# Attention part of a decoder layer: low context parts and the input's addition by accumulating transfers, three context buffers, another order of the norm statistics

## What is computed

```python
x = _layernorm(x + rwkv(x, ...))            # 4 layers with a scan over time
x = _layernorm(x + xattn(x, ctx, ...))      # the part that the change touches
x = _layernorm(x + experts(x, ...))         # 8 experts, gated

def xattn(x, y):                            # 16 heads of 16 channels
    q = softmax(heads(x @ Wq.T + bq))       # over the 16 channels of a head
    k = softmax(heads(y @ Wk.T + bk))
    v = heads(y @ Wv.T + bv)
    D_inv = 1 / sum(q * sum(k over rows))
    out = q + einsum(q, einsum(k, v)) * D_inv
    return out @ Wp.T + bp
```

## The kernel before

| slot n % 4 | DVE between `block_diagonals` and `k_normalise` | DVE behind `low_context` |
|---|---|---|
| 0 | `add_input(n / 4)`: L1164 `x<-x,xin`, then `stats(1, ...)` L1149; in slot 0 the five instructions of `output_bias` ahead of it | `rsqrt(1, ...)` (five instructions, L1155 to L1159), then `denominators` (L1187 `drec`, from slot 4 on) |
| 1 | | `attend`, `q_arguments` |
| 2 | `q_normalise` | in slots 6, 8 and 10 `low_weights` (L1212), in 10 and 14 `low_x2` (L1207) |
| 3 | `add_attention` with its statistics | `rsqrt(2, ...)` |

## Time and profile before

### The profile page before, as it was taken

One profiled execution on the slowest core, in us unless ns is written; L12 is line 12 of the kernel. 1 busy time (PEld: TensorE's weight loads), 2 busy tenths in 40 slices (PEclk: granted clock), 3 DMA queues, 4 the chain that ended last, 5 costly groups with the idle time before them and its releaser, 6 DMA issues.

```text
span 1833.9 us, 27225 instructions
## 1 busy us (share of the span) xinstructions
PE 1733.1 (95%) x10508; PEld 1517.4 (83%) x10508; DVE 1242.6 (68%) x1918; ACT 978.5 (53%) x1505; POOL 3.6 (0%) x26
## 2 busy tenths in 40 slices
PE   3599999999999998998999999999999999999997
PEld 1378888787888788888899889998999989999896
DVE  7999999999999855888544444444454544444446
ACT  4688898898989873444533333233333332333323
POOL 0000000000000000000000000000000000000000
PEclk9799999999999998999999999999999999999999
DMA  4000010001000002111111011110101001020001
GB/s 143 1 24 18 12 47 18 7 7 61 3 12 29 0 29 89 44 55 45 55 35 35 1 35 35 34 34 0 34 34 34 18 16 34 34 74 0 1 1 41
DMA packets 34702, 56.59 MB, mean 31 GB/s; under 512 B 3030, under 2 KB 20412, under 8 KB 33596
## 3 DMA queue, kind: packets, MB, share of 16 engines
q1 hardware_dynamic: 34620, 55.47, 9.3%
HBM read 51.79 MB, written 3.67 MB: 30 GB/s over the span
## 4 chain that ended last, share of the span: by engine, by line
PE 70%; DVE 24%; ACT 3%; issue 2%; DMA 0%; SPq 0%; ACTq 0%; DVEq 0%
PE fbank L1941 33%; PE fbank L1963 17%; PE pair L842 5%; PE pair L802 4%; PE pair L827 3%; DVE kfl L425 2%; PE proj L1435 2%; PE pair L812 2%; DVE st L272 2%; DVE aa L374 1%; DVE bb L370 1%; DVE pp L356 1%; PE pair L792 1%; PE qbanks L1471 1%; DVE x L413 1%
## 5 line engine op out<-in xcount | busy, mean ns | idle before, releaser
L1763 DVE TENSOR_TENSOR hf<-sil,fbank 128x512 f32<-128x512 f32 (+1 forms) x256 | 158.8, 620 | 479.2 <-PE fbank L1941 407.6
L1868 ACT ACTIVATE sil<-fbank 128x512 f32<-128x512 f32 (+1 forms) x256 | 139.2, 544 | 615.1 <-PE fbank L1941 615.1
L1941 PE MATMUL fbank<-xh,wh 128*128 128x512 f32 (+1 forms) x1024 | 289.9, 364 | 1.2 <-ACT sil L1868 1.2
L1941 PE MATMUL fbank<-xl,wh 128*128 128x512 f32 (+1 forms) x1024 | 289.1, 364 | 0.0
L1941 PE MATMUL fbank<-xh,wl 128*128 128x512 f32 (+1 forms) x1024 | 289.0, 363 | 0.0
L1963 PE MATMUL fbank<-wl,hh 128*128 128x256 f32 x896 | 250.4, 279 | 0.0
L1963 PE MATMUL fbank<-wh,hh 128*128 128x256 f32 x896 | 250.3, 279 | 0.0
L1963 PE MATMUL fbank<-wh,hl 128*128 128x256 f32 x896 | 250.2, 279 | 0.0
L1941 PEld LDWEIGHTS fbank<-xl,wh 128*128 128x128 f32 x1024 | 184.6, 189 | 30.8
L1941 PEld LDWEIGHTS fbank<-xh,wl 128*128 128x128 f32 x1024 | 184.5, 189 | 30.4
L1941 PEld LDWEIGHTS fbank<-xh,wh 128*128 128x128 f32 x1024 | 180.5, 189 | 27.8 <-ACT sil L1868 1.6
(11 more groups left out here) (239 smaller groups left out, 3106.0 us busy)
## 6 DMA issues: line engine op xcount, KB each, us to landing
raw<-in_w_gate SPq DMA_DIRECT2D x16, 512.0 KB, 3.9
raw<-in_w_up SPq DMA_DIRECT2D x16, 512.0 KB, 4.8
raw<-in_w_down SPq DMA_DIRECT2D x16, 512.0 KB, 5.7
raw<-in_w_ck SPq DMA_DIRECT2D x4, 1024.0 KB, 4.7
raw<-in_w_cv SPq DMA_DIRECT2D x4, 1024.0 KB, 4.8
raw<-in_ctx_t SPq DMA_DIRECT2D x4, 750.0 KB, 6.3
ct<-in_ctx_t SPq DMA_DIRECT2D x4, 750.0 KB, 4.9
x<-in_x SPq DMA_DIRECT2D x4, 448.0 KB, 6.8
```

The costliest lines, as they stand in the source:

```text
L1763: dve.tensor_tensor(hf[i][:, 0:w], sil[i][:, 0:w], banks(e, t, f)[1][:, 0:w], ALU.mult).then_inc(hf_ready, 1)
L1868: act.activation(sil[f % 2][:, 0:w], banks(e, t, f)[0][:, 0:w], ACT.Silu).then_inc(sil_ready, 1)
L1941: ins = pe.matmul(banks(e, t, f)[k][:, 0:w], m[h][:, o:o + P], a[:, b, columns(c)], start=i == 0, stop=i == 3 * CB - 1)
```

## The change

- The low part of a context is no longer subtracted on DVE. ACT writes the negated high part into `ctl`, and GpSimd issues a transfer that adds the context from HBM onto it (`accum_op=ADD`).
- `cth` and `ctl` have three buffers instead of two. `high_context(n + 3)` stands where `high_context(n + 2)` stood, with `high_context(2)` ahead of it in slot 0.
- `xin` and its loads are gone: GpSimd issues transfers that add the input from HBM onto x in SBUF. DVE's `add_input` becomes `input_stats`, which waits for that transfer and takes the statistics.
- In slots 0, 4, 8 and 12 the statistics stand behind `k_normalise`, and `denominators` stands ahead of `rsqrt(1, ...)`.
- SP waits for `cth_ready` where it waited for `ctl_ready`; `kvbd` takes the place of `xin` in SBUF; the last phase's `eps` waits for `num_done`.

```diff
-        xin = [sb(f"xin{i}", [T, G, C]) for i in range(2)]
+        kvbd = sb("kvbd", [P, 2 * G, CB, P])
...
-        cth, ctl = ([sb(f"{n}{i}", [P, CB, S + 1], F32R) for i in range(2)] for n in ("ach", "acl"))
+        cth, ctl = ([sb(f"{n}{i}", [P, CB, S + 1], F32R) for i in range(3)] for n in ("ach", "acl"))
...
         def gpsimd(pool):
...
+            def add_context(s):
+                pool.wait_ge(minus_ready, s + 1)
+                if s >= 3:
+                    pool.wait_ge(ctl_in[s % 3], 16 * (s // 3))
+                pool.dma_start(ctl[s % 3][:, :, 0:S], io["ctx_t"][:, :, s * S:(s + 1) * S].bitcast(F32R),
+                               accum_op=ALU.add).then_inc(ctl_in[s % 3], 16)
+
+            def add_input(c):
+                if c >= 2:
+                    pool.wait_ge(sum_in[c % 2], 16 * (c // 2))
+                pool.dma_start(x[:, c * G:(c + 1) * G, :], xv[:, c * G:(c + 1) * G, :], accum_op=ALU.add)\
+                    .then_inc(sum_in[c % 2], 16)
+
+            add_context(0)
+            add_context(1)
+            pool.wait_ge(g["x_done"], 2 * STEPS)
+            add_input(0)
+            for s in range(2, B):
+                add_context(s)
+                if s % 2 == 0 and s // 2 < GROUPS:
+                    add_input(s // 2)
...
         def sync(sp):
...
             sp.wait_ge(g["x_done"], 2 * STEPS)
-            load_x(0)
-            load_x(1)
             sp.dma_start(g["wrt"][:], io["wrt"]).then_inc(g["wrt_in"], 16)
...
-                sp.wait_ge(ctl_ready, CG * (j - 1))
+                sp.wait_ge(cth_ready, CG * (j - 1))
                 load_context(sp, io, ct, ct_in, j)
...
         def vector(dve):
...
-            def add_input(c):
-                dve.wait_ge(xin_in[c % 2], 16 * (c // 2 + 1))
-                dve.tensor_tensor(chunk(c), chunk(c), xin[c % 2][:], ALU.add).then_inc(sum_done, 1)
-                dve.wait_ge(sum_done, c + 1)
+            def input_stats(c):
+                dve.wait_ge(sum_in[c % 2], 16 * (c // 2 + 1))
                 stats(1, c)
...
-                    if i == 0 and c1 is not None:
-                        add_input(c1)
                     if i == 2 and c1 is not None:
                         q_normalise(c1)
                     if i == 3 and c2 is not None:
                         add_attention(c2)
                     k_normalise(n)
-                    if n + 2 < B:
-                        low_context(n + 2)
+                    if i == 0 and c1 is not None:
+                        input_stats(c1)
+                    if i == 0 and c2 is not None:
+                        denominators(c2)
                     if i == 0 and c1 is not None:
                         rsqrt(1, c1)
-                    if i == 0 and c2 is not None:
-                        denominators(c2)
...
         def scalar(act):
...
-                if s >= 2:
-
-                    act.wait_ge(proj_done, s - 1)
-                act.activation(cth[s % 2][:, :, 0:S], ct[s // CG % 2][:, :, c0:c0 + S], ACT.Copy).then_inc(cth_ready, 1)
+                if s >= 3:
+
+                    act.wait_ge(proj_done, s - 2)
+                act.activation(cth[s % 3][:, :, 0:S], ct[s // CG % 2][:, :, c0:c0 + S], ACT.Copy).then_inc(cth_ready, 1)
+                act.wait_ge(cth_ready, s + 1)
+                act.activation(ctl[s % 3][:, :, 0:S], cth[s % 3][:, :, 0:S], ACT.Copy, scale=-1.0).then_inc(minus_ready, 1)
...
-                    if n + 2 < B:
-                        high_context(n + 2)
+                    if n == 0:
+                        high_context(2)
+                    if n + 3 < B:
+                        high_context(n + 3)
...
         def tensor(pe):
...
-                pe.wait_ge(ctl_ready, s + 1)
+                pe.wait_ge(ctl_in[s % 3], 16 * (s // 3 + 1))
```

## The result

| | kernel before | changed kernel |
|---|---|---|
| median of 20 runs, us | 1838.33 | 1841.78 |
| lowest, highest | 1835.23, 1839.4 | 1838.97, 1845.22 |
| profiled execution (span) | 1835.63 (1833.9) | 1843.36 (1841.6) |

The ratio is 1.0021 with a 95% interval of 1.0014 to 1.0027: 3.5 us slower, 2.9 us above the predicted 1838.9 and inside the range. 1.0 us of the 7.7 is there before the attention part begins and is no part of the change (0.6 of it by the first instruction on DVE).

What follows compares the result with a forecast made beforehand. PE was taken to bound the kernel, idle about 20 of 190 us. Queues +0.1, input +1.0 and clock 0 gave 1.1 on the profiled 1835.63, 1836.7; 2.2 more to the median made 1838.9 us, range 1832.5 to 1847.

Steps and rivals of the forecast that it cites:

- Slot 0: First attention slot: key quotient starts 2.46 us earlier, PE turns x at 716.5 instead of 717.88; gain 1.4 us.
- Slot 4: denominators ahead of rsqrt makes DVE stand at drec, so PE turns x at 758.45 instead of 756.91; loss 1.54 us.
- Slots 8, 12 and 11: Slots 8 and 12: earlier projection, given back by the order, loss 0.5 us each; slot 11: earlier maximum top, gain 1.0.
- The low parts' transfers: Sixteen accumulating transfers of 375 KB on GpSimd's queue, 8 us each, with enough lead: no cost, bounds 0 to 6.8 us.
- the rival: Slower, by the low parts: 14 us from negation to landing, PE waits before projections of contexts 13 and 5; 1845.7, chance 0.13.
- The input's first part: Slot 0: accumulation issued from 702.59, wanted by DVE at 711.5, taken to land at 712.5; cost 1.0 us.
- The clock: PE's granted clock in slots 0 and 1: gain 2.2 us if no fall, about 2.4 cost if longer; taken as 0.
- The forecast's side: Whole kernel within 0.2% (3.7 us) of the kernel before; chance 0.54.
- The faster one: Freed DVE time reaches PE, moved denominators costs nothing, clock stays up in slot 0: -6.2 us, 1831.6; chance 0.16.
- Input late: Slot 0: the input's first accumulation lands 6 us late, at 717.5, holding DVE at input_stats(0); 1843.9 us, chance 0.17.
- low parts late: Low parts take 14 us instead of 8, so PE waits before projections of contexts 13 and 5; 1845.7 us, chance 0.13.

Runs made afterwards that it cites:

- experiment 8: Experiment 1 with high_context(n + 2) again, so low parts' transfers have a slot less of lead; 1842.67 us beside 1836.63 for the kernel before.
- experiment 1: The changed kernel with denominators put back behind rsqrt(1, ...) in slots 4, 8 and 12; 1833.23 us beside 1837.68 for the kernel before.
- experiment 4: The changed kernel with twelve idle products on PE before its wait for x in slots 4, 8 and 12; 1836.8 us beside 1837.68.
- experiment 5: Experiment 1 with the router's and expert's weights and next context issued only after the input's first part lands; 1832.17 us beside 1836.63.
- experiment 12: The changed kernel again, unedited, on another chip; 1842.82 us beside 1836.85 for the kernel before.
- experiments 9 to 12: Experiment 5 with statistics of groups 1 to 3 earlier (1832.56 us); experiment 1 with input added on DVE (1832.8); the first with slot 0 filled (1828.86); experiment 12 (1842.82).
- experiment 3: The kernel before with denominators ahead of rsqrt and nothing else; 1848.51 us beside 1837.68.
- experiment 2: The kernel before with only the change's order of addition, statistics and denominators, low parts still on DVE; 1848.42 us beside 1837.68.
- experiment 7: Experiment 5 with 24 idle products on PE in slot 0 before the turn of x; 1830.41 us beside 1836.63 for the kernel before.

## Why the prediction came out as it did

**Slot 0** was right to a tenth. With the 1.0 us of start-up taken off, the product starts at 711.6 and the turn at 716.5, as predicted; the fewer idle microseconds before the product came back behind it, 3.28 before the turn.

**Slot 4** was right: turn at 758.40 with the 0.19 by which the product was late taken off, 758.45 predicted. The mechanism is in the rows: DVE stands at `drec` until PE's sums are done, and the five small instructions are queued behind that wait.

**Slots 8, 12 and 11** were right: +0.4 (product of slot 7 to turn of slot 8) and +0.4 instead of +0.5 each, and -1.0. The time that left DVE bought nothing in sum, as said, because each freed piece lies in front of a wait that ends at the same time as before or is given back by the order.

**The low parts' transfers** were right in cost, nothing, and taken too slow: 5.6 us in the median, where 8 was taken and twice the plain load would have been 9 to 15. The issues from 674 to 900 us (KB each, median us from issue to landing), the input's first part by itself, and GpSimd's own time for the first two issues in the part:

```profile
acl<-in_ctx_t POOLq DMA_DIRECT2D x16, 375.0 KB, 5.6
...
x<-in_x POOLq DMA_DIRECT2D x1, 448.0 KB, 6.6
...
703.88 1.24 POOL L1035 DMA_DIRECT2D x<-in_x  x1 [22.64 <-DVE x L463]
...
711.07 1.10 POOL L1028 DMA_DIRECT2D acl<-in_ctx_t  x1 [5.96 <-ACT acl L1335]
```

No projection waited for them. Single ones took longer than the 10 us that the prediction names as a sign of being wrong, 11.1 for a low part and 10.1 for a part of the input, early in the part beside other loads; they had more lead than that. With one slot less of lead the kernel loses 10.5 us (experiment 8), so it is the lead that keeps them free. The Trainium skill's page "SBUF — State Buffer", section "SBUF: two separate sides", on which the rival leaned for a cause, says that GpSimd's descriptor writes stall beside DVE's two-port copies. No run here shows such a stall: sixteen of the twenty issues took 1.05 to 1.24 us. The four others stand right behind another issue and took 1.61 to 1.91, within 0.01 us of that in experiment 1's profile.

**The input's first part** was taken 1.0 us late and in this profile wasn't late at all: 703.88 + 6.6 = 710.5, while DVE came to it at 712.47. In other kernels' profiles it was (9.9 us in experiment 1 with a DVE wait of 1.27, 10.6 in experiment 4); what that costs in the median isn't shown, and experiment 5 puts it near nothing. The pages' estimate, 4.1 us for 448 KB, put together from "DMA: Bandwidth & Descriptors", section "Anatomy of one DMA — SWDGE (gpsimd) path", and "Collectives: The Full Stack", section "The bandwidth ceiling: the fold count and why AG ≠ RS ≠ AR", of the Trainium skill (which gives the halved rate for the reduce-scatter of a ring of cores, not for a transfer like this one), is too short here: 6.0 us even with the other loads held back (experiment 5). The measurement decides.

**The clock is the step that failed.** The prediction took 0 for it, with bounds of -2.2 and +2.4, and looked for it in slots 0 and 1 alone, where the clock was low already. There it moved little (+0.6 up to slot 4). But its own queue model made three new waits of 1.3 us in slots 4, 8 and 12, between two that were there, 0.65 for `drec` and 1.01 for `xt`, and it priced them only as waits. In both profiles of the changed kernel the clock fell behind two of the three: 2.8 us in slots 4 and 5, 1.6 in slots 8 and 9, more than the waits themselves. The rows to size this were in hand: the same turn and projection take 1.76 and 2.05 us at the low level, 0.93 and 1.12 at the high one. Put on slots 4, 8 and 12 that is a bound of 0 to 6.6 us instead of nothing.

The medians fit that. The queues give about 0 (+0.1 predicted, -0.1 read off), and with the waits filled the changed kernel's loss of 3.5 us becomes a gain of 0.9 (experiment 4), which can't be told from no change. The executions say the same by their mean granted clock. Of the changed kernel's twenty, the five with 0.982 or 0.983 took 1838.97 to 1839.84 us, the fifteen with less 1840.48 to 1845.22; its fastest in experiment 12, at 0.984, took 1836.82. The kernel before is alike: of the 22 executions beside experiments 9 to 12, the nine with 0.983 or 0.984 took 1835.05 to 1836.64, the others, at 0.981 or 0.982, 1836.47 to 1838.8. Its profiled execution is one of the first kind, 0.984. By this reading, which rests on means and not on traces, the 2.2 us that the prediction added to come from the profile to the median are a clock term of before, and one reason why the medians lie 3.5 us apart and the profiles 7.7.

The measured time lies in the range, but that is in part luck: in the profile the forecast's +1.0 for the input was nothing and its 0 for the clock was 6.7. The forecast's side, within 0.2%, is missed by little: the ratio is 1.0021, and its interval holds 1.002.

**The rivals.** The faster one fell with its condition: `denominators` is not free, since PE hadn't finished the sums when DVE came to them. Without the moved `denominators`, the kernel is 4.5 us faster than before (experiment 1), near the sum of the steps that are left, 1.4 + 2 x 0.8 + 1.0 = 4.0. Input late and low parts late: not in this kernel, as above. The slower side came by a mechanism that none of the rivals named.

**What stays open.** Clock terms are read from one or two executions of a kernel. The fall at about 903 to 915 us, 1.7 us of the profiled difference, lies in the experts' part; before has a smaller one there (0.89 from 900 to 915 us, 0.79 in the changed kernel), and what sets its size wasn't tested. It doesn't hang on the falls in slots 4 to 9: experiment 3's profile has it without them. Nor is it settled why a wait of 1.32 us is followed by a fall in slots 4 and 8 of the changed kernel and not in slot 12, and in experiment 2's profile and not in experiment 3's.

## What to carry to other kernels

Time taken off a busy engine is worth only what the waits for that engine lose: follow each freed piece to the next wait, and look what stands behind every instruction that waits for PE, because a step that is queued behind it is paid for at full length by whoever waits for that step. Price each new idle piece of PE twice, as a wait and as a possible fall of the clock for the work behind it, with durations of the same instructions at both levels. An accumulating transfer needs its lead, here some 6 us in the median and up to 11 beside other loads (15 in experiment 5); give it a buffer more before taking the addition off an engine.

## What the runs showed of the hardware

- An idle piece of 1.3 us on PE, between two of 0.65 and 1.01 us that alone brought no fall in before, can cost more behind it than it lasts: 2.8 us in slots 4 and 5, where the granted clock was 0.64. Products with no use, put into the wait, made the kernel 4.3 us faster (experiment 4); 24 of them in a wait of 3.3 us made it 1.8 us faster (experiment 7).
- The same kernel can fall into or out of such a loss from one execution to the next: 1841.26 us at a mean granted clock of 0.982 and 1847.1 to 1849.4 at 0.977 or 0.978 in experiment 3. A single profile can hide such a term or show too much of it.
- An accumulation from HBM onto SBUF took 5.6 us in the median for 375 KB and, for the input's first 448 KB, 6.0 us with the other loads held back, within the 4.6 to 7.5 of the plain loads in the earlier trace rows, and 6.6 to 10.6 with 1.5 MB of plain loads beside it. An issue keeps GpSimd 1.1 to 1.2 us, and 1.6 to 1.9 right behind another.
